# Two attention stages and the ternary tail between them, written as one program instead of two

## The reference

```python
x = x + tanh(g_xattn[0]) * heads(LN(x), ctx, ctx, mask, ...)      # 16 heads of 32, softmax, sigmoid gate
x = x + tanh(g_ffn[0])   * ternary(LN(x), weight, bias)           # rows quantised to 255 steps
x = x + tanh(g_xattn[1]) * features(LN(x), ctx, ctx)              # per tile: V @ sigmoid(Q.T @ K / sqrt(128))
x = x + tanh(g_ffn[1])   * moe(LN(x), ...)                        # 16 experts, 4 for each row, and a shared one
```

## Time and profile before

| | us |
|---|---|
| time of 3 runs: median (lowest to highest) | 1336.06 (1332.77 to 1338.27) |
| the profiled execution, device time | 1338.2 |
| its span | 1336.5 |
| TensorE busy | 1224.6 (92%) |
| VectorE / ScalarE / GpSimd busy | 712.1 / 551.9 / 433.5 |
| first attention and ternary layer | 0 to about 470 |
| second attention | about 470 to 582.6 |
| routing and experts | from 582.9 |

### The profile page before, as it was taken

The page is one execution under the profiler, slowest core; times in us unless marked ns, Lnnn a source line. Parts: engine busy times, 40 slices in busy tenths (PEclk is TensorE's granted clock), DMA queues, the critical chain, the costliest instruction groups (busy, mean ns, idle before and its releaser), DMA issues. The chain is left out here.

```text
span 1336.5 us, 26105 instructions
## 1 busy us (share of the span) xinstructions
PE 1224.6 (92%) x7848; PEld 1029.7 (77%) x7849; DVE 712.1 (53%) x1401; ACT 551.9 (41%) x1362; POOL 433.5 (32%) x521
## 2 busy tenths in 40 slices
PE   6998999999897579959999999899999999999995
PEld 5876777778776357745677777789999888899995
DVE  5667556556556479974466664643224553424241
ACT  4544445345345168853221111443334553434342
POOL 1102211210211365551002664234444434444433
PEclk9999999999999779979999999999999999999998
DMA  9100000000000021132100131476445566555554
GB/s 329 31 17 19 17 1 19 17 1 18 1 1 2 0 64 39 46 123 96 57 0 1 65 129 40 153 184 144 78 78 135 143 178 153 138 94 129 85 137 71
DMA packets 54907, 101.36 MB, mean 76 GB/s; under 512 B 5158, under 2 KB 22054, under 8 KB 54838
## 3 DMA queue, kind: packets, MB, share of 16 engines
q0 software_dynamic: 15824, 37.76, 14.9%
q1 hardware_dynamic: 39014, 62.70, 14.4%
HBM read 73.96 MB, written 26.48 MB: 75 GB/s over the span
## 5 line engine op out<-in xcount | busy, mean ns | idle before, releaser
L1873 PE MATMUL t_H<-m_W,t_xT 128*128 128x352 f32 x1632 | 281.5, 328 | 7.3 <-DVE m_W L1951 5.8
L1873 PEld LDWEIGHTS t_H<-m_W,t_xT 128*128 128x128 f32 x1632 | 262.9, 189 | 10.0 <-DVE m_W L1951 8.2
L1841 POOL DMA_INDIRECT out_dram<-t_ys,t_sid x68 | 109.5, 1610 | 223.8 <-ACT t_ys L1902 107.7
L1918 ACT ACTIVATE t_sl<-t_H 128x352 f32<-128x352 f32 x68 | 31.5, 463 | 174.9 <-PE t_H L1873 174.9
L601 ACT ACTIVATE pr<-pr 128x128 f32<-128x128 f32 x256 | 76.1, 298 | 55.3 <-DVE pr L762 54.0
L66 PE MATMUL t_Y<-m_W,t_hT 128*128 128x512 f32 (+1 forms) x207 | 88.1, 426 | 5.0 <-issue 3.1
L1996 DVE TENSOR_TENSOR t_hT<-t_TH,t_hT 128x384 fp32r<-128x384 f32 x68 | 37.8, 556 | 101.6 <-ACT t_hT L1939 100.5
L1972 DVE TENSOR_TENSOR t_h<-t_H,t_sl 128x352 f32<-128x352 f32 x68 | 35.6, 524 | 103.5 <-ACT t_sl L1918 103.5
L1902 ACT ACTIVATE t_ys<-t_Y,t_wcol 128x512 f32<-128x512 f32 x69 | 47.2, 685 | 94.7 <-PE t_Y L68 94.7
L68 PE MATMUL t_Y<-m_W,t_hT 128*128 128x512 f32 (+1 forms) x207 | 82.1, 397 | 0.0
L67 PE MATMUL t_Y<-m_W,t_hT 128*128 128x512 f32 (+1 forms) x207 | 81.9, 396 | 0.0
(11 more groups left out here) (446 smaller groups left out, 3278.2 us busy)
## 6 DMA issues: line engine op xcount, KB each, us to landing
m_raw<-in_L_ffn_w_dram SPq DMA_DIRECT2D x28, 704.0 KB, 5.9
m_raw<-in_L_ffn_w_dram SPq DMA_DIRECT2D x14, 512.0 KB, 4.1
aCX<-in_ctx_dram SPq DMA_DIRECT2D x20, 256.0 KB, 2.6
rows_d<-before_w SPq DMA_DIRECT2D x17, 256.0 KB, 2.0
CT<-in_ctx_dram SPq DMA_DIRECT2D x8, 512.0 KB, 3.7
X<-in_x_dram SPq DMA_DIRECT2D x4, 1024.0 KB, 12.6
out_dram<-X SPq DMA_DIRECT2D x3, 1024.0 KB, 4.3
m_raw<-in_L_ffn_sw_dram SPq DMA_DIRECT2D x4, 704.0 KB, 5.8
```

The source lines that it names most:

```text
L1841: pool.indirect_dma_start(out=m["out_rows"][:, :], out_offset=bass.IndirectOffsetOnAxis(ap=sid[:, b:b + 1], axis=0), in_=ys[:, b, :], in_o ...
L1873: x_ = pe.matmul(bk[b % 2][:, 0:I], xT[:, b % 2, jx, k, :], W13[:, jw, k, j, :], start=k == 0 and jx == jw, stop=k == KC - 1 and jx == 1)
```

## The change

1. `attention_features` is gone. Its work is now words of the same plan: `cx` (load of the context), `ta` (scales), `an` (norm), `qh` and `ks` (splits), `aT` (transposes), `aS` (scores), `ag` (sigmoids), `ap` and `aO` (products, the last with the update of X and its statistics). It is unrolled, and counts in the same semaphores. Its buffers lie in those of the first attention: q and k in W["k"], the transposed context in W["v"], sigmoids in W["q"] and kT, the context in CT and qT; scores use the banks SC, O and REC, the sum the banks M.
2. The last group of tiles has an order of its own, which begins the second attention, and the ternary tail stands between the first steps of it.
3. Scales: `ta.0` and `ta.1` make mean and rstd for the second attention (tiles 0 to 11, then 12 to 15), `ta.2` and `ta.3` those for routing (tiles 0 to 7, 8 to 11). `experts` makes only those of tiles 12 to 15, after its first two norms, and does the gate's transposes and split after two tiles.
4. Softmax: VectorE no longer subtracts. It makes `neg`, the negative scaled maximum of four columns, which exp takes as bias, reading SC itself. The sums get a maximum with 0.5 ahead of the reciprocal. The banks SC are free for the next scores after the exps.

```diff
-        plan += steps("sf.-4 sf.-3 st.-2 st.-1 ra.-1 rb.-1 rd.-1 u.-2 uT.-2 u.-1 fm.-2 uT.-1 fm.-1 sf.-2 sf.-1", NG)
+        plan += steps(
...
+            "sf.-1 v.2 bc.1 pv.3 on.1 oT.1 pT.8 ta.0 g.2 Sa.5 pT.9 Sb.5 sm.10 sm.11 an.0 qh.0 ks.0 "
+            "oP.1 st.0 pv.4 g.3 pT.10 Sa.6 pT.11 rc.2 Sb.6 sm.12 sm.13 an.1 qh.1 ks.1 "
+            "bc.2 pv.5 on.2 oT.2 st.1 pT.12 v.3 ra.0 Sa.7 pT.13 Sb.7 sm.14 sm.15 "
+            "oP.2 aT.0 rb.0 pv.6 aT.1 rd.0 u.0 pT.14 uT.0 aS.0.0 u.1 pT.15 aS.0.1 rc.3 fm.0 ag.0.0 bc.3 pv.7 uT.1 ag.0.1 on.3 oT.3 "
+            "aS.0.2 fm.1 oP.3 ", NG - 1)
+        between = {0: "sf.-4", 1: "st.-2", 2: "sf.-3", 3: "st.-1", 5: "ra.-1", 6: "rb.-1", 7: "rd.-1 u.-2", 9: "uT.-2", 10: "u.-1",
+                   12: "fm.-2", 13: "uT.-1", 16: "fm.-1", 18: "sf.-2", 20: "sf.-1", 22: "ta.1", 36: "ta.2", 52: "ta.3"}
+        MS = NB * KC
+        for m in range(MS):
+            b, n = m // KC, m % KC
+            text = [between.get(m, "")]
+            if m + 3 < MS:
+                text += [f"aS.{(m + 3) // KC}.{(m + 3) % KC}"]
+            if m + 2 < MS:
+                text += [f"ag.{(m + 2) // KC}.{(m + 2) % KC}"]
+            if n == 0 and b + 2 < NB:
+                text += [f"an.{b + 2}"]
+            if n == 2 and 1 <= b + 1 < NB and b:
+                text += [f"aT.{b + 1}"]
+            text += [f"ap.{b}.{n}" if n < KC - 1 else f"aO.{b}"]
+            if n == KC - 1 and b + 2 < NB:
+                text += [f"qh.{b + 2} ks.{b + 2}"]
+            if n == KC - 1 and b + GB < NB:
+                text += [f"cx.{b + GB}"]
+            plan += steps(" ".join(text), NG)
+        fresh = [slice(0, 3 * GB), slice(3 * GB, NB), slice(0, 2 * GB), slice(2 * GB, 3 * GB)]
...
-                            wait(pe, s_out, 4 * t)
+                            wait(pe, p_exp, 2 * t)
...
                     elif kind == "sm":
                         act.wait_ge(s_out, 2 * t + 2)
+                        wait(act, t_fill, at(T_KINDS, ("pT", t - 2)))
+                        wait(act, o_norm, 2 * (t // HQ) - 3)
...
-                            pp, at_ = pr[:, t % 2, slot, :], t % HQ * HQ + slot
-                            i = act.activation(pp, pp, ACT.Exp, scale=SCALE0, accum_out=sums[:, t // HQ % 2, at_:at_ + 1])
+                            at_ = t % HQ * HQ + slot
+                            i = act.activation(pr[:, t % 2, slot, :], SC[t % 2][:, slot * S:(slot + 1) * S], ACT.Exp, scale=SCALE0,
+                                               bias=neg[:, t % 2, slot:slot + 1], accum_out=sums[:, t // HQ % 2, at_:at_ + 1])
...
-                        dve.tensor_tensor(pr[:, t % 2, :, :], bk, mx[:, t % 2, :].unsqueeze(2).to_broadcast([P, HQ, S]),
-                                          ALU.subtract).then_inc(s_out, 1)
+                        wait(dve, p_exp, t - 1)
+                        dve.tensor_scalar(neg[:, t % 2, :], mx[:, t % 2, :], MASKED / 10, -SCALE0, ALU.max, ALU.mult).then_inc(s_out, 1)
...
-                        dve.reciprocal(rec[:, t % 2, :], sums[:, t % 2, :]).then_inc(o_norm, 1)
+                        dve.tensor_scalar(some[:, t % 2, :], sums[:, t % 2, :], 0.5, None, ALU.max).then_inc(some_ok, 1)
+                        dve.wait_ge(some_ok, t + 1)
+                        dve.reciprocal(rec[:, t % 2, :], some[:, t % 2, :]).then_inc(o_norm, 1)
...
-                row_scale(dve, c, scales, powered, 1e-5)
                 norm(0)
                 norm(1)
-                dve.wait_ge(g_hi, 1)
...
+                row_scale(dve, c, scales, slice(3 * GB, NB), 1e-5)
                 for t in range(NB):
+                    if t == 2:
+                        dve.wait_ge(g_hi, 1)
```

More of the change, by code:

```diff
@@ L41 @@
 META = AT_TRIPS + 1
[L44 to L61, removed]
 def mm3(pe, out, lhs, rhs, first, last):
@@ L91, in program, with row_scale @@
             parts[f"passed_{e}"] = top.enter_context(nc.semaphore(f"passed_{e}"))
-        attention_heads_and_ternary(nc, parts, x, g_x, g_f, fw, fb, ctx_in, mask, norm_w, wq, wk, wv, wo, wg)
-        attention_features(nc, parts, ctx_in)
+        attention_and_ternary(nc, parts, x, g_x, g_f, fw, fb, ctx_in, mask, norm_w, wq, wk, wv, wo, wg)
         experts(nc, parts, gate_w, ebias, w1, w2, w3, sw1, sw2, sw3, out)
[L97 to L104, removed]
+def row_scale(dve, c, done, tiles, eps):
+    t, bst, mean = c["tmp16"][:, :, tiles], c["bst"][:, tiles, :], c["mean"][:, tiles]
+    diff, squares, var, r1 = (t[:, k, :] for k in range(4))
+    n = 0
     def step(*instrs):
@@ L118, in row_scale, with row_power, attention_and_ternary @@
     step(dve.scalar_tensor_tensor(out=var, in0=squares, scalar=1.0 / D, in1=r1, op0=ALU.mult, op1=ALU.add))
[L119 to L145, removed]
+    dve.tensor_scalar(t[:, 4, :], var, eps, None, ALU.add).then_inc(done, 1)
+def row_power(pool, c, done, tiles, powered):
+    pool.wait_ge(done, 7)
+    pool.tensor_tensor(c["rstd"][:, tiles], c["tmp16"][:, 4, tiles], c["nhalf"][:, tiles], ALU.pow).then_inc(powered, 1)
+def attention_and_ternary(nc, c, x, g_x, g_f, fw, fb, ctx_in, mask, norm_w, wq, wk, wv, wo, wg):
     X, identF = c["X"], c["identF"]
@@ L302, in col_of, with summed, projected @@
             return (j // 2 * 2 + r % 2) * HQ + r // 2 * 2 + j % 2
[L304 to L306 removed]
+        def summed(eng, m):
+            b, n = m // KC, m % KC
+            if n == KC - 1:
+                eng.wait_ge(m_fill, at(M_KINDS, ("aO", b)))
+            else:
+                eng.wait_ge(as_used, (KC - 1) * b + n + 1)
+        def projected(eng, n, t):
+            eng.wait_ge(m_fill, at(M_KINDS, (n, t, KC - 1) if n in "qk" else (n, t)))
         with nc.Block() as block:
@@ L1236, in _, with gate @@
             def _(pe):
-                pe.wait_ge(g_in, 32)
-                for k in range(KC):
-                    i = pe.transpose(G[:, k * E:(k + 1) * E], gw[:, k * P:(k + 1) * P], c["identF"][0:E, 0:E])
-                i.then_inc(gt, 1)
-                pe.matmul(L[:, 0:E], c["onesF"][0:1, :], b1[:, :], start=True, stop=True).then_inc(bias_ps, 1)
+                def gate():
+                    pe.wait_ge(g_in, 32)
+                    for k in range(KC):
+                        i = pe.transpose(G[:, k * E:(k + 1) * E], gw[:, k * P:(k + 1) * P], c["identF"][0:E, 0:E])
+                    i.then_inc(gt, 1)
+                    pe.matmul(L[:, 0:E], c["onesF"][0:1, :], b1[:, :], start=True, stop=True).then_inc(bias_ps, 1)
                 def logit(g):
@@ L1355, in _ @@
                     i.then_inc(t_fill, 1)
+                    if t == 1:
+                        gate()
                     if t % GB == 1 and t > GB:
```

336 lines of the change are left out of this document (154 added, 182 removed), and 4 rows, old and new, of the table d.

## The result

The changed kernel takes 1314.03 us (median of 4 runs, 1312.92 to 1316.72) against 1337.16 for the kernel before beside it (4 runs, 1332.77 to 1338.72): ratio 0.9834, 95% interval 0.9809 to 0.9859. Repeated later it took 1314.95 (5 runs) with the ratio 0.9834 again, 0.9810 to 0.9858. The gain is 23 us where 32 were forecast; 1314 lies in the range, ten us above the predicted 1304.

A forecast was written before the change was run, and what follows sets the result against it. TensorE was taken to bound the second attention at 6.18 us a tile, VectorE nearly as full. Terms -8 - 24.9 + 1 = -31.9 took 1338.2 to 1306.3 us, 1304 beside the median; range 1291 to 1320.

The forecast's parts named there:

- Part 1: First attention: maximum as bias of exp relieves VectorE, shortening TensorE's waits, mainly for `u`; -8 us, ends 0 and 12.
- the end of 12 us: First attention, best case of the bias change: two short half-clock stretches following the waits for `u` vanish as well.
- Part 2: Merge up to the last oP: it ends 0.9 us later, plus 2 us for half clock after two waits.
- Part 3: Last oP to second attention's end: TensorE's 96.7 us plus 7 for VectorE's additions (ends 0 and 14); TensorE's part ends 24.9 earlier.
- TensorE's sum of 96.7: Second attention: 16 tiles at 6.18 us, less work done ahead and the loop's vanished prefetch, plus the tail's uT and fm.
- behind a power that waits for VectorE stand the k splits: GpSimd's queue in the second attention: splits needed four steps later stand behind a waiting power; GpSimd's added work fits.
- Part 4: Routing stage: first norms start 4 us earlier, worth 0 beside the weight load; +1 us taken, ends -3 and +3.
- TensorE stays fed: Rival, second attention: late norms get cheaper on VectorE, the tail hides, clock stays up; 1292 us, chance 0.12.
- VectorE is the bound to the end: Rival, second attention: all 15.7 us of VectorE's additions come back, some tail operations slow beside GpSimd; 1318 us, chance 0.18.
- The merge moves no start: Rival: a wait in the written order holds the second attention where it began; 1328 to 1334 us, chance 0.04.
- Half clock throughout: Rival "Slower": short TensorE waits bring 1.2 GHz in the second attention; up to +77 us, 1380; chance 0.04.
- The uT waits, the exps and the norm of routing: Signs: first attention's uT waits 1 us shorter, exps 0.09 longer; routing's norm(0) 4 us earlier against the stage's start.

The follow-up runs named there:

- the bias alone: Kernel before with only the first attention's softmax changed (maximum as bias of exp), no merge: 1323.72 us, ratio 0.9917.
- the two comparisons: Merge added to the kernel before (old softmax kept, 1326.78 us), and merge added to the kernel with only the bias change (1323.72 us, giving the kernel after).
- the second profile: Kernel after, unchanged, profiled again beside the later repeat runs: 1315.03 us.
- 26 us less on VectorE: Kernel after with VectorE's low part of `as` made for 128 of 512 columns, output less exact: stretch 105.0 us instead of 116.4, total 1326.27.
- one word: Kernel after with GpSimd's power `ta.1` at step 24 instead of 22, behind tile 7's k split: 1309.60 us, ratio to before 0.9799.

## Why the prediction held, point by point

- **Part 1**, -8: the mechanism is confirmed and its size was low. Each wait for `u` shrank by 1.1 us, where 1.0 was worked out from the earlier trace rows; exps went from 298 to 377 ns (+0.08; +0.09 was taken from the earlier trace rows); the waits for `pr` hardly moved (4.3 us before, 3.7 with the bias alone), and no wait for the SC banks appeared. From the first oP to the last, TensorE's idle time fell from 27.8 to 20.3 us, 7.5 less where 8 were forecast. But the trace gives -13.7 and the times -10.4, and what is on top is the clock: half clock fell from 17.0 to 10.2 us, which is worth up to 3.4 us; I had put this in the end of 12 us and not in the value. Of the rest of the trace's 13.7 us, 1.1 lie ahead of the first oP and some 2 in small pieces that I have not told apart. The exps of the kernel after, 60 to 340 (the kernel with the bias alone has the same mean over its 256, 378 ns):

```profile
L688 ACT ACTIVATE pr<-SC,neg 128x128 f32<-128x128 f32 x176 | 61.8, 377 | 25.7 <-DVE neg L897 25.7
```

- **Part 2**, +0.9 and +2: low. It is +5.9 and +7.0 in the two comparisons. The places were right (uT.0 waits 3.1 us where 3.4 were forecast, and behind the sigmoids 3.0 where 2.9 were), but the clock was half for 6.9 us from 422.9 on, across the first of them, and for 3.4 us behind the second, and the wait of pT.14 ahead of both (1.8, for ScalarE's copy of the transposed context) was not in the layout. That the last oP came within 1.6 us of the forecast is luck: part 1 gave 5.7 us more than forecast and part 2 cost 4.1 more.
- **Part 3**, the second attention as 96.7 + 7: **the term that was mis-sized**. What stands above TensorE's sum of 96.7 is 19.7 us and not the 7 given for VectorE. By its own rows the prediction could have seen it: VectorE has 93.6 us of its own in that stretch and gets 15.7 more; less some 6 us done ahead of the last oP, that is 103, exactly the length that I forecast, so the forecast left VectorE not one us of idling, where it had idled 5 even in the even loop. In the trace it is busy 107.1 us and idles 9.3 (107.2 and 7.8 in the second profile). The sum for TensorE was carried through; the one for VectorE was made only for the first steps. Seen from TensorE, the 12.7 us are 5.6 more of idling (12.6 where 7 were forecast) and 7.1 more of being busy (103.8 for 96.7). For these part 3 had no term: 8.4 busy us were at half clock, which costs 4.2 by estimate (half of them), and 2.9 are not told apart. Seen from the causes, I can name two: the contention that spread to the low parts (+3.4, if all of it reaches TensorE), and the wait behind the power on GpSimd with its half clock (3.0 without the half clock, 4.4 with it, as in this profile). The prediction had named the second ("behind a power that waits for VectorE stand the k splits") and priced it at nothing. The rest, 4.9 us, stays open. The wait of 3.7 us for `u` and the 6.8 us of half clock beside it may be most of it: the wait stood there with 26 us less on VectorE too.
- **Part 4**, +1: right in its main point, the early scales are worth 0. The stage is still 3.5 us shorter than in the profile of before (1.5 in the second profile of the kernel after); but the kernel with the bias alone, which has the old stage, takes 23.0 us for the part that was 25.1, so before's profile was a long one there, and the +1 is not seen.
- **The rivals.** "TensorE stays fed" is out: the norm did get cheaper, as it said, and the low parts dearer by more. "VectorE is the bound to the end" was the nearer one in time (1318); its mechanism holds up to 497 and not beyond, since TensorE is busy 97% from 501.5 on. "The merge moves no start" is out. Half clock throughout is out: outside 10.2 us of the stretch TensorE had 1.00.
- **Signs.** The uT waits, the exps and the norm of routing came as written. That TensorE would wait for the low part of `as` 5 to 10 us did not: 1.3 us. Here the full engine made TensorE wait longest where the order puts its longest chain, which is `u`, and behind the power, and not where most of its time goes.

## What to carry to other kernels

When a stage is put beside another, add up the list of every engine over the new stretch, not only the bound engine's, and let none come out with less idle time than it has now. Then look at each queue that is served in order for an instruction that waits for the full engine: what stands behind it and is ready should go ahead, which was worth more here (3.0 to 4.4 us of the stretch for one word) than moving a wait for the full engine itself by the order (1 us at most). Where two engines get in each other's way, an operation that shows no loss may lie beside the other engine's work all the same and merely begin first; another order takes that from it.

## What the runs showed of the hardware that I had not expected

- The same fp32 norm of 128x512 from memory to memory takes 0.54 us on VectorE alone, 0.83 to 1.53 when it begins while a cast or `tensor_tensor` of 512 columns runs on GpSimd (second attention of the kernel after), and 2.07 to 3.04 on GpSimd (mean 2.33 of 14; spans on GpSimd are rough).
- A `tensor_tensor` of VectorE, 128x512, with both inputs in SBUF takes 0.68 us with GpSimd idle and also when it begins first. When it begins within a cast or `tensor_tensor` of 512 columns on GpSimd it ends 0.54 to 0.55 us after that one (21 of 21) and takes up to 1.78 us. With one input in PSUM VectorE's operations took 0.68 to 0.75 in all 29 cases of the stretch.
- The same wait can leave the clock alone or halve it. In the two profiles of the kernel after, the wait of 2.96 us at 497.1 is followed by 3.4 us at 1.2 GHz, and the wait of 2.95 us at 498.8 by none. One of 2.3 us in the routing stage has 3.4 us of it behind it in both (from 682.4 in the first), where the profile before kept 2.4 GHz.
- GpSimd's power of two columns takes 0.70 us in the first attention and 1.21 in the merged stretch; four columns take 1.39 us, eight 2.02.
